# State-space tiles: folding y without TensorE, output projection in half rows, and a new order within a tile

## The reference, cut to what matters

```
delta = softplus(dlt @ Wdt.T + bdt)                  # step product, 64 inputs
h_t   = exp(delta*A[e,n]) * h_(t-1) + delta*B_t[n]*u # n = 0..15, scan over t
y_t   = sum_n C_t[n]*h_t[n] + u*D                    # u = z product, 512 inputs
out   = x + gate * ((act_mx*(y1 + y2)) @ Wf.T + skip terms)
```

## Time and profile before

| | |
|---|---|
| three runs | 6279.13, 6286.2 and 6286.43 us, median 6286.2 |
| profiled execution | 6282.06 us, its span 6280.0 us |
| granted clock of TensorE, mean over the span | 0.976 |
| busiest engine over the span | PE, 5784.1 us (92%) |

### The profile page before, as it was taken

One profiled execution on the slowest core, in us unless ns is written; L12 is line 12 of the kernel. 1 busy time (PEld: TensorE's weight loads), 2 busy tenths in 40 slices (PEclk: granted clock), 3 DMA queues, 4 the chain that ended last, 5 costly groups with the idle time before them and its releaser, 6 DMA issues.

```text
span 6280.0 us, 135632 instructions
## 1 busy us (share of the span) xinstructions
PE 5784.1 (92%) x58208; PEld 3025.7 (48%) x58208; DVE 4223.3 (67%) x5708; ACT 2914.6 (46%) x4943; POOL 2868.7 (46%) x921
## 2 busy tenths in 40 slices
PE   8899979997889999859979999999999999999998
PEld 2455545553455555524435545454454544545454
DVE  1166635552555555546469889798897988979786
ACT  0022212221555555622156656566665656656564
POOL 0001001000000000014258878798897988979786
PEclk9999989998999999979989999999999999999999
DMA  5200020001000000023321111111110111101110
GB/s 205 77 29 31 22 72 31 30 22 61 10 16 16 16 16 16 8 80 137 135 88 49 61 54 40 43 54 61 51 62 24 52 62 49 64 22 53 62 42 27
DMA packets 142967, 321.67 MB, mean 51 GB/s; under 512 B 25769, under 2 KB 27050, under 8 KB 132154
## 3 DMA queue, kind: packets, MB, share of 16 engines
q1 hardware_dynamic: 142402, 313.39, 14.5%
HBM read 238.46 MB, written 74.89 MB: 50 GB/s over the span
## 4 chain that ended last, share of the span: by engine, by line
PE 40%; POOL 5%; issue 2%; ACT 2%; DVE 1%; DMA 0%; SPq 0%; POOLq 0%; DVEq 0%
PE wide L2008 13%; PE wide L1992 12%; PE wide L1966 7%; POOL sc_state L1841 3%; PE wide L2029 3%; PE wide L1951 2%; PE wide L2021 2%; ACT sc_parts L1904 1%; PE wide L1973 1%; POOL sc_diag L1810 1%; DVE sc_state L2122 1%; DMA sc_w_out<-in_wfT 0%; POOL sc_gated L1822 0%; DVE sc_y_sum L2093 0%; POOL sc_resid L1828 0%
## 5 line engine op out<-in xcount | busy, mean ns | idle before, releaser
L2122 DVE TENSOR_TENSOR_SCAN sc_state<-sc_decay,wide 128x512 f32<-128x512 f32 x2048 | 2338.9, 1201 | 346.5 <-PE wide L1992 346.5
L1841 POOL TENSOR_TENSOR sc_state<-sc_state,sc_c_rows 128x2048 f32<-128x2048 f32 x512 | 2327.4, 4551 | 507.0 <-DVE sc_state L2122 507.0
L1921 ACT ACTIVATE sc_decay<-sc_delta,sc_neg_a 128x512 f32<-128x512 f32 x2048 | 1424.4, 718 | 822.9 <-DVE sc_state L2122 822.9
L1992 PEld LDWEIGHTS wide<-sc_diag,sc_du_t 64*64 64x64 f32 x32768 | 915.0, 133 | 654.7 <-DVE sc_state L2122 317.3
L2008 PE MATMUL wide<-sc_state,sc_half 64*64 64x512 f32 x8192 | 1071.3, 593 | 76.3 <-ACT sc_parts L1904 60.3
L1992 PE MATMUL wide<-sc_diag,sc_du_t 64*64 64x128 f32 x32768 | 1113.9, 273 | 3.8 <-DVE sc_state L2122 3.1
L1328 DVE CUSTOM_DVE_ANT_0 l_prob<-wide,l_mask_add 128x512 f32<-128x512 f32 x512 | 340.5, 684 | 294.7 <-PE wide L1198 294.7
L1966 PE MATMUL wide<-sc_xn_t,sc_w_z 128*128 128x512 f32 x1024 | 508.9, 620 | 0.0
L1113 ACT ACTIVATE l_prob<-l_prob,l_s_max 128x512 f32<-128x512 f32 x512 | 366.0, 715 | 275.0 <-DVE l_s_max L1328 274.7
L460 PE MATMUL wide<-l_w,l_xn_t 128*128 128x512 f32 x1024 | 445.1, 592 | 1.6 <-PEq L84 1.6
L1209 PE MATMUL wide<-l_ident,l_prob 128*128 128x128 f32 x2048 | 298.3, 283 | 103.8 <-DVE l_prob_t L1337 90.6
...
## 6 DMA issues: line engine op xcount, KB each, us to landing
...
sc_w_z<-wz_tiles SPq DMA_DIRECT2D x128, 256.0 KB, 2.7
...
```

The costliest lines, as they stand in the source:

```text
L1841: pool.tensor_tensor(state[quad % STATES][:, :, :], state[quad % STATES][:, :, :], c_rows[(r * 4 + q) % ROWS][:, :, :], ALU.mult).then_inc ...
L1921: act.activation(decay[step % DECAYS][:, :], delta[slot % 2][:, :], ACT.Exp, scale=neg_a[:, s, m, n:n + 1]).then_inc(decay_ready, 1)
L1992: last = pe.matmul(to[cols_to, k, :, :], du_t[slot % 2][rows, k, cols_to], diag[rows, c, k, :, :], start=True, stop=True)
L2122: dve.tensor_tensor_scan(state[quad % STATES][:, step % 4, order], decay[step % DECAYS][:, order], pair[:, i, order], 0.0, ALU.mult, ALU.a ...
```

## The change

- `fold`, `parts` and `drain_sums` are gone. `sums` now writes bank `acc[i]` (even states of a pair to `acc[0]`, odd ones to `acc[1]`, with the row halves on different partitions). DVE adds `acc[0]` to y (`add_sums`, after chunk 3 of the next tile). ACT copies the two partition halves of `acc[1]` crosswise into `s_bank` (`swap_sums`), and DVE adds that (`add_swapped`, after chunk 4).
- `dt_product` becomes two products in 64x64 tiles, which share their rows and take a half of the columns each.
- `output` works in eight pieces an element, each half a row (256 columns), one in each of slots 1 to 8, four products in each of chunks 6 and 7. The `resid` loads and stores of SP and the adds of POOL move with it: loads at slots 0, 2, 4 and 6, adds at slots 3, 5, 7 and 9, stores at slots 4, 6, 8 and 10. POOL still adds whole rows.
- The order on PE, ACT and DVE within a tile is new. In it `sums` of chunks 4 and 5 run back to back behind the turn, `scaled_input` moves behind chunk 4, and the second half of the z product to chunk 3.

The diff, without the renamed semaphores (`y_added`, `dl_full`, `o_full` and `o_drained` now count two a tile or piece) and SP's part:

```diff
@@ -1845,8 +1839,8 @@
                         build(r + 1, 2 * q + 1)
                     if q == 3 and slot >= 1 and where(slot - 1)[1] == 1:
                         gating(slot - 1)
-                    if q == 1 and s == 0 and b >= 1 and 2 <= m <= 5:
-                        output(b - 1, m - 2)
+                    if q == 1 and b >= 1 and slot % 16 in (3, 5, 7, 9):
+                        output(b - 1, (slot % 16 - 3) // 2)
                 gating(SLOTS - 1)
                 for t in range(TT):
                     output(B - 1, t)
@@ -1896,18 +1890,26 @@
                     act.activation(du_t[slot % 2][:, :, :].rearrange("p k n -> p (k n)"), s_bank, ACT.Copy
                                    ).then_inc(du_t_ready, 1)
 
-                def drain_sums(slot):
+                def swap_sums(slot):
                     act.wait_ge(summed, 16 * (slot + 1))
-                    if slot >= 1:
-                        act.wait_ge(fold_full, 2 * slot)
-                    for i in range(2):
-                        act.activation(parts[:, i, :], acc[i], ACT.Copy).then_inc(parts_ready, 1)
+                    if slot + 2 < SLOTS:
+                        act.wait_ge(delta_ready, slot + 3)
+                    else:
+                        act.wait_ge(y_added, 2 * slot)
+                    for g in range(2):
+                        act.activation(s_bank[g * 64:(g + 1) * 64, :], acc[1][(1 - g) * 64:(2 - g) * 64, :], ACT.Copy
+                                       ).then_inc(swapped, 1)
 
                 softplus(0)
                 softplus_end(0)
                 direct(0)
                 turned_du(0)
                 for chunk in range(CHUNKS + 8):
+                    slot, c = (chunk - AHEAD) // 8, (chunk - AHEAD) % 8
+                    if chunk >= AHEAD and c == 3 and slot >= 1:
+                        swap_sums(slot - 1)
+                    if chunk >= AHEAD and c == 5 and slot + 1 < SLOTS:
+                        turned_du(slot + 1)
                     if chunk < CHUNKS:
                         slot = chunk // 8
                         b, s, m = where(slot)
@@ -1927,12 +1929,8 @@
                         softplus(slot + 1)
                     if c == 1 and slot + 1 < SLOTS:
                         softplus_end(slot + 1)
-                    if c == 3 and 1 <= slot:
-                        drain_sums(slot - 1)
-                    if c == 3 and slot + 1 < SLOTS:
+                    if c == 4 and slot + 1 < SLOTS:
                         direct(slot + 1)
-                    if c == 4 and slot + 1 < SLOTS:
-                        turned_du(slot + 1)
 
             @block.tensor
             def _(pe):
@@ -1944,12 +1942,12 @@
                     r, i = slot // 8, m % 2
                     if m == 0:
                         pe.wait_ge(dlt_loaded[r % 2], (r // 2 + 1) * 32)
-                    if slot >= 2:
-                        pe.wait_ge(y_added, slot - 2)
                     if slot >= 1:
                         pe.wait_ge(du_t_ready, slot)
-                    pe.matmul(s_bank, wdt[i * R:(i + 1) * R, s, m // 2, :], dlt[r % 2][i * R:(i + 1) * R, :],
-                              start=True, stop=True).then_inc(dl_full, 1)
+                    for g in range(2):
+                        half_of = slice(g * 64, (g + 1) * 64)
+                        pe.matmul(s_bank[half_of, :], wdt[i * R:(i + 1) * R, s, m // 2, half_of],
+                                  dlt[r % 2][i * R:(i + 1) * R, :], start=True, stop=True).then_inc(dl_full, 1)
 
                 def z_product(slot, ks):
                     b, s, m = where(slot)
@@ -1969,6 +1967,8 @@
 
                 def turn(slot):
                     pe.wait_ge(du_ready, slot + 1)
+                    if slot >= 2:
+                        pe.wait_ge(y_added, 2 * (slot - 1))
                     for k in range(4):
                         last = pe.transpose(s_bank[:, k * P:(k + 1) * P], du[:, k::4], ident[:, :])
                     last.then_inc(turned, 1)
@@ -2000,34 +2000,26 @@
                     if h == 0:
                         pe.wait_ge(weighted, quad + 1)
                         if q == 0 and slot >= 1:
-                            pe.wait_ge(parts_ready, 2 * slot)
+                            pe.wait_ge(swapped, 2 * slot)
+                            pe.wait_ge(y_added, 2 * slot - 1)
                     for i in range(2):
                         n = 2 * h + i
                         for g in range(2):
                             to = (g + i) % 2
-                            ins = pe.matmul(acc[g][to * 64:(to + 1) * 64, :], half[g * 64:(g + 1) * 64, :],
+                            ins = pe.matmul(acc[i][to * 64:(to + 1) * 64, :], half[g * 64:(g + 1) * 64, :],
                                             state[quad % STATES][g * 64:(g + 1) * 64, n, :],
                                             start=(q == 0 and h == 0), stop=(q == 3 and h == 1))
                             if h == 1:
                                 ins.then_inc(summed, 1)
 
-                def fold(slot):
-                    pe.wait_ge(parts_ready, 2 * (slot + 1))
-                    if slot + 2 < SLOTS:
-                        pe.wait_ge(du_t_ready, slot + 3)
-                    else:
-                        pe.wait_ge(y_added, slot)
-                    for g in range(2):
-                        pe.matmul(s_bank[g * 64:(g + 1) * 64, :], half[:, :], parts[:, g, :], start=True, stop=True
-                                  ).then_inc(fold_full, 1)
-
-                def output(b, t, ks):
+                def output(b, piece, ks):
+                    t, h = piece // 2, piece % 2
                     if 0 in ks:
                         pe.wait_ge(gated_ready, (b + 1) * ET)
-                        pe.wait_ge(o_drained, b * TT + t)
+                        pe.wait_ge(o_drained, b * 2 * TT + piece)
                     for k in ks:
-                        last = pe.matmul(z_bank, gated[:, k, t * P:(t + 1) * P], w_out[:, k, :],
-                                         start=(k == 0), stop=(k == ET - 1))
+                        last = pe.matmul(z_bank[:, 0:256], gated[:, k, t * P:(t + 1) * P],
+                                         w_out[:, k, h * 256:(h + 1) * 256], start=(k == 0), stop=(k == ET - 1))
                     if ET - 1 in ks:
                         last.then_inc(o_full, 1)
 
@@ -2038,28 +2030,33 @@
                 for chunk in range(-1, CHUNKS + 8):
                     if chunk + 1 < CHUNKS:
                         inputs(chunk + 1)
-                    if chunk >= 4 and (chunk - 4) // 2 < QUADS:
-                        sums((chunk - 4) // 2, chunk % 2)
                     if chunk < 0:
                         continue
                     slot, c = chunk // 8, chunk % 8
+                    b, s, m = where(slot)
+                    if c <= 3 and slot >= 1:
+                        sums(4 * slot - 2 + c // 2, c % 2)
+                    if slot == SLOTS:
+                        continue
                     if slot + 1 < SLOTS:
                         if c == 0:
                             dt_product(slot + 1)
-                        if c in (1, 2):
-                            z_product(slot + 1, range(2 * c - 2, 2 * c))
-                        if c == 4:
+                        if c in (1, 3):
+                            z_product(slot + 1, range(c - 1, c + 1))
+                        if c == 5:
                             turn(slot + 1)
-                    if c == 6 and slot >= 1:
-                        fold(slot - 1)
-                    b, s, m = where(slot)
-                    if 1 <= b < B and s == 0 and 1 <= m <= 4 and c >= 4:
-                        if c == 4:
+                    if c == 5:
+                        sums(4 * slot, 0)
+                        sums(4 * slot, 1)
+                    if c >= 6:
+                        sums(4 * slot + 1, c - 6)
+                    if 1 <= b and 1 <= slot % 16 <= 8 and c >= 6:
+                        if c == 6:
                             pe.wait_ge(du_ready, slot + 2)
                             pe.wait_ge(z_direct, slot + 2)
-                        output(b - 1, m - 1, range(2 * c - 8, 2 * c - 6))
-                for t in range(TT):
-                    output(B - 1, t, range(ET))
+                        output(b - 1, slot % 16 - 1, range(4 * c - 24, 4 * c - 20))
+                for piece in range(2 * TT):
+                    output(B - 1, piece, range(ET))
 
             @block.vector
             def _(dve):
@@ -2089,24 +2086,32 @@
                     dve.scalar_tensor_tensor(du[:, :], z_bank, bzc[:, i:i + 1], delta[slot % 2][:, :],
                                              ALU.add, ALU.mult).then_inc(du_ready, 1)
                     if s == 1:
-                        dve.wait_ge(y_added, slot - 7)
+                        dve.wait_ge(y_added, 2 * (slot - 7))
```

(41 more changed lines are left out.)

46 lines of the change are left out of this document (20 added, 26 removed).

## The result

| | before | after |
|---|---|---|
| median of four runs, us | 6283.46 | **6208.52** |
| lowest to highest, us | 6279.13 to 6286.43 | 6204.45 to 6209.52 |
| profiled execution, its span, us | 6282.06, 6280.0 | 6208.52, 6206.6 |
| ratio of after to before, 95% interval | | 0.9878, 0.9866 to 0.989 |
| first to last step size of the last stage, us | 3005.57 | 2927.13 |

The change saves 1.2%. In the profiled executions it saves 73.4 us. The last stage itself, taken from the step size (`step_size` on DVE) of the first tile to that of the last, is 78.4 us shorter; in this execution of after it began 4.8 us later, though the code ahead of it is the same. All later statements on the stage use this length, which does not depend on where it begins.

A forecast was written before the change was run, and what follows sets the result against it. PE was taken to lead, DVE 1.3 to 1.9 us behind, DVE then bounding ordinary tiles. Element 0 saves 8, elements 1 to 7 11.5 each: 88.5 off 6282.06 gives 6193.5, stated as a 6196 median; range 6120 to 6272.

The forecast's parts named there:

- Point 1: The fold leaves PE, with its shape turns: 1.01 + 0.10 + 0.04 = 1.15 us a tile less.
- point 6: Output projection in eight half-row tiles: 24.5 us each, eight tiles 206.8 to 196.45, -10.4 for each of seven elements.
- Point 2: Step product on PE as two 64x64 products: 0.88 instead of 1.19, gain 0.31 us a tile.
- Point 3: PE's wait for ACT's copies before `sums`, 0.68 us a tile, goes to nothing, covered by 4.4 us of other work.
- Point 4: DVE's second add of y costs 0.58; its work, 20.24 (s = 0) and 20.91 (s = 1), bounds ordinary tiles.
- Point 5: DVE waits 0.45 for chunk 3's inputs and 0.35 for the new add's `sums`; ordinary tiles 21.04 and 21.71 us.
- Point 7: POOL's work is unchanged; an element's last tile and the next one's first gain nothing, waiting for POOL.
- Point 8: SP's moved resid loads and stores cost nothing; the end of the program put at 0, bounds -2 and +4.
- the banks of the sums: Rival: both row halves writing one `acc` bank run one after the other, 0.86 more a `sums` group; 6927 us, 8%.
- Half rows that pay for their loads: Rival: half-row weight loads partly not hidden (+96), or step products one after the other (+110); 6292 to 6306 us, 7%.
- The case in which DVE takes it all in ordinary tiles: Rival: DVE or latencies keep ordinary tiles at 21.96, output tiles 1 us longer; 14 us left, 6272 us, 13%.
- the case of more gain: Rival: the 0.8 us of DVE waits and PE's 0.55 vanish, 74 us more gain; 6122 us, 8%.

The follow-up runs named there:

- both: Changed kernel with the add of acc[0] moved behind chunk 4's scans and the z product halves moved to chunks 2 and 3; 6147.82 us, ratio 0.9779.
- Both, du between: The kernel of "both" with du (the scaled input) computed between the two adds of y instead of behind them; 6133.28 us, ratio 0.9757.

## Why the prediction was right, and where not

The forecast was 6196 in a range of 6120 to 6272, with 0.83 on faster; 6208.5 was measured. The forecast case came in; its terms were together 1.1 us an element too good. The range is wide, 152 us, and would also have held a gain of only 14, so the account below goes by tiles.

- **Point 1, the fold: -1.15.** Not undone alone. What speaks for it is the output tile of "both", in which PE never waits: 23.87 less the two bursts of 2.06 of point 6 is 19.75, and 21.96 - 0.36 - 0.68 - 1.15 is 19.77.
- **Point 2, the step product: forecast -0.31, measured -0.36** in two runs. So it costs 0.83, a little less than a `sums` group, and its records alternate with those of the following `inputs`. That the `inputs` fill the half of the array left free is an inference from these records.
- **Point 3, the wait for ACT's copies: right.** 60.3 us in before, none in after. That the new order, and not the lost fold, took this wait away is argued from the cover and not shown. The order was not at its best: the adds and the half of z, both moved, give 59.3 more.
- **Point 4, DVE becomes the bound of ordinary tiles: right.** PE's waits for scans went from 3.1 to 77.1 us, and 16 scans with 4 or 5 other operations leave DVE no gap once its two waits are removed.
- **Point 5, the two waits of DVE: right in place.** Forecast 0.45 and 0.35, idle shown 0.39 and 0.26; tiles 21.04 and 21.71 forecast, 21.14 and 21.80 measured. "Both, du between" splits the miss of 0.09 to 0.10. DVE's work without waits is 20.41 and 21.07 there, and point 4 had 20.24 and 20.91: **the 0.11 taken off for each wait was too much, and the term came out 0.17 too small.** The two waits then are 0.73 and not 0.80. So the tile came out as near as it did because the two misses partly cancel.
- **Point 6, the output tiles: 24.5 right (24.49), but its sum off.** I gave 0.45 more to one tile; two have it (24.99 and 25.07), since in slot 7 PE, DVE and ACT already prepare the first tile with s = 1. Eight tiles took 197.0 and not 196.45. **The sentence that failed is "The gain is that the output's PE time is spread over tiles in which DVE has slack".** Full rows on four tiles, with the rest of the change, give 9.0 of the 10.0 us in these eight tiles, and 0.4 more in the tile behind them. The -10.4 of this point came in because 1.15 + 0.31 + 0.68 leave PE in every one of the eight tiles, and an output tile is bound by PE. I had put both edits into one difference of eight tiles, so the sum could not tell which of them it was worth.
- **Point 7, POOL at the set change: right.** Forecast no gain for the two tiles: 45.26 before, 45.46 after. In the four faster runs that keep the builds it is never under 45.4, and it falls only where the builds are cut or moved.
- **Point 8, SP and the end: right, by two terms that cancel.** From POOL's last weighted quad to the end 47.2 us in before, and 46.9 in after. The gating of the last y ends its wait 2.5 earlier without the fold, and each of the four rows of output takes 0.4 to 0.6 longer in two pieces (8.60 from one add of POOL to the next, 7.98 before). TensorE's clock was at 0.5 for 13.7 us of this stretch in before and for 10.2 in after.
- **The sum.** 88.5 forecast for the stage, 78.4 measured. Element 0 gave 5.7 and not 8; the others 10.4 and not 11.5. Of this 1.1, 0.4 is the output tiles (0.5 more in after, less 0.17 that before also pays behind its last piece), about 0.5 the 0.09 in six ordinary tiles, and 0.2 the set change.

The rivals: the banks of the sums would have shown as `sums` groups of 1.7; they start 0.85 apart from what follows, with both row halves on one bank and different partitions. This agrees with the Trainium skill, "PSUM — Partial Sum Buffer" (bank collisions), which narrows a collision to the same 32 partitions, and not with the flat statement of "TensorEngine Tiling (Array Packing)", Gotcha 1. Half rows that pay for their loads would have shown as 1.92 plus some; it is 1.92. So the rule of the Trainium skill, "TensorE: Matmul & The Clock Gate", Part 3, does not hold for these passes. The prediction also made this rival too dear: it priced all 896 half-row passes, but 448 full-row passes with such loads stood in the measured time before. Only 448 loads are new. At the same price of about 107 ns from the Trainium skill (the same title, LDWEIGHTS) they are an estimated 48 us and not 96, which would have taken about half of the gain and not all of it. The case in which DVE takes it all in ordinary tiles fell by 0.82 a tile with s = 0 and 0.16 with s = 1, and the case of more gain was there to be had, though not in this kernel: it is "both, du between", whose stage is 68.8 us shorter than after's.

Left open: the fold was not put back alone, so its 1.15 rests on the sum of the output tile above. What lets TensorE's clock fall in some intervals and not in others like them was not tried. The order of before as a whole was not tried without the fold; it was varied only in the adds and the half of z.
